# Dividing the attention probabilities by their row sums before they are transposed, on GpSimd and ScalarE, instead of scaling the output after the value product

## The chip, the cores and the metric

The kernel runs on one core of one Trainium2 chip, as one program and one launch. The metric is the device time of that core in microseconds, the lower the better; the time given for a kernel is the median of its runs. All five engines of the core take part: TensorE (PE in the rows; its weight loads are PEld), VectorE (DVE), ScalarE (ACT), GpSimd (POOL) and SyncE (SP, which only issues DMAs here).

## The reference, cut to what matters

The input is x, 2 batches of 512 tokens of width 256. The reference applies a layer norm with modulation, a first attention with a sliding window of 128 and sinks, a residual, a second layer norm with modulation, and then a block with a causal attention and a mixture of 8 experts (top 2). Both attentions have 32 query heads of width 64 in 8 groups of 4, each group sharing one key and one value head. The change touches the causal attention alone:

```
scores = einsum("bhqd,bhkd->bhqk", q, k) / sqrt(64)
scores = where(causal, scores, lowest)
attn = softmax(scores, axis=-1)            # exp, divided by the sum of the row
out = einsum("bhqk,bhkd->bhqd", attn, v)
return out.transpose(0, 2, 1, 3).reshape(b, s, 2048) @ wo
```

The division by the row's sum may be made on the probabilities (before the product with v) or on the output (behind it): a row of the output has one divisor per head, and both give the same numbers but for rounding.

## The kernel before

The attention is cut into 128 **units** u. A unit is one tile of 128 queries of one batch for the four heads of one group. Units 0 to 63 are the windowed attention, units 64 to 127 the causal one; `windowed(u)` tells them apart. Within four units the query tile t = u mod 4 runs from 0 to 3, and a causal unit has `keys(u)` = t + 1 blocks of 128 keys. Projections of the next groups (`ahead(u)`: q, k, v or features) are done between the units, in most steps of a segment but not in all; in the last twelve steps there are none.

Every engine has its own in-order program, written by hand as a loop over **steps**. In step u of the causal part (`step_causal`; `step` on GpSimd) the parts of several units are in flight:

- TensorE: `scores(u, j)` for the four heads j into psS; `turn_probs(u-2, k)` transposes the four heads' probabilities of key block k into psX; `values(u-2, k)` multiplies them with v into psO (its last block comes in the next step); `turn_scale(u-3)` transposes the two halves of rdenx into the other half of psO; `out_project(u-5)`; and `project(ahead(u))`. The first transposes of a step, `turn_probs(u-2, 0)`, come right behind `scores(u, 0)`.
- VectorE: `mask_max(u, j)` masks the scores, writes them to pbuf and takes the row's maximum; `probs_lo(u-2, k)` makes pTl, the low part of the transposed probabilities; `denominator(u-2)` takes the reciprocal of the sums (rden); `scale_out(u-3)` multiplies psO by rS into oS.
- ScalarE: `exp_head(u, j)` in place in pbuf with the row's sum; `probs_hi(u-2, k)` copies psX to pTh, the high part; `scale_of(u-3)` copies the transposed divisors to rS; `out_hi(u-4)` makes oh.
- GpSimd: `out_low(u-4)` makes ol = oS - oh; `low_weights(u)` makes the low part of the next weights; `spread(u-1)` copies rden four heads wide into rdenx; `gate_rows` in steps 84 to 88 is other work at the end of a step.

So a divisor takes this way before: reciprocal on VectorE, copy to 128x256 on GpSimd, two transposes on TensorE, a copy on ScalarE, and the multiplication on VectorE. The wait of `turn_probs(u, 0)` is for the four exponentials of its unit (a_exp), which ended a step earlier. Four buffers of probabilities (u mod 4) are in use in turn.

## Time and profile before

| | us |
|---|---|
| median of three runs | 1074.36 |
| the three runs | 1067.90, 1074.36, 1074.54 |
| the profiled execution | 1067.51 |
| its span, first to last instruction | 1065.9 |

In the profiled execution the causal steps run from about 407 to 800 us. Over the whole span TensorE is busy 91%, VectorE 74%, ScalarE 71% and GpSimd 44%. The granted clock of TensorE is given as a share of 2.4 GHz: 0.958 in the mean, 1.00 between 400 and 812 us. Times in the rows are microseconds from the span's start. A row of a timeline gives start and duration, engine, source line, operation, written tile <- read tiles and the number of merged instructions; in brackets stands the idle time of the engine just before it, and who ended it. Matmuls are pipelined, so that the duration of a row of four transposes (0.60) is longer than the time in which the next work can start (0.44 on the chain).

### The profile page before, as it was taken

The numbers are of one execution on the slowest core, as the hardware profiler recorded it, in microseconds if no ns is written. First come the engines' busy times: TensorE is split into PE (matmuls) and PEld (weight loads), VectorE is DVE, ScalarE is ACT, GpSimd is POOL, SyncE is SP. The second block draws the span as 40 slices with busy tenths as digits, with TensorE's granted clock in tenths as the row PEclk, the third lists the DMA queues.
The fourth block names the chain that finished last, engine by engine and source line by source line (L and its number), as shares of the span: only waits on it lengthen the run. The fifth ranks groups of instructions, "written<-read, shape, count | busy, mean of one in ns | idle before, by whom it ended". The sixth has DMA issues, their size and how long they took to land.

```text
span 1065.9 us, 22953 instructions
## 1 busy us (share of the span) xinstructions
PE 967.2 (91%) x6862; PEld 904.5 (85%) x6862; DVE 790.7 (74%) x2308; ACT 752.6 (71%) x2122; POOL 465.0 (44%) x550
## 2 busy tenths in 40 slices
PE   5679899999889899999999999999997689999991
PEld 3469899998789799988999999999987589999991
DVE  6679988889889677777776777677774766666646
ACT  3358787888788688788888778887784455665541
POOL 4347567868555443533354233222221862222243
PEclk9889999999999899999999999999998699999996
DMA  8789778896455586546456654645301385565314
GB/s 185 173 213 281 198 198 260 221 233 170 119 140 152 164 189 179 129 115 174 119 129 180 148 139 130 148 120 149 72 10 48 124 283 161 165 171 168 106 58 116
DMA packets 146059, 166.18 MB, mean 156 GB/s; under 512 B 79194, under 2 KB 100714, under 8 KB 140816
## 3 DMA queue, kind: packets, MB, share of 16 engines
q1 hardware_dynamic: 129440, 143.58, 52.1%
q0 software_dynamic: 3712, 11.16, 3.3%
q10 hardware_dynamic: 12784, 9.97, 3.0%
q8 instruction: 56, 0.92, 0.4%
q14 instruction: 67, 0.55, 0.2%
HBM read 105.88 MB, written 58.79 MB: 154 GB/s over the span
## 4 chain that ended last, share of the span: by engine, by line
PE 57%; DVE 18%; issue 9%; ACT 8%; DMA 3%; POOL 3%; SPq 0%; ACTq 0%; DVEq 0%; POOLq 0%
PE psO L1086 15%; PE psS L1053 10%; PE psX L1063 9%; PE psY L1102 6%; PE psP L985 6%; ACT wgt_hi L1319 3%; DVE pbuf L1735 3%; DVE gated L2065 2%; PE psO L1069 2%; PE psP L1015 2%; DVE pTl L1757 2%; POOL xg L892 2%; DVE den L1749 1%; PE psP L998 1%; DVE tmp L1703 1%
## 5 line engine op out<-in xcount | busy, mean ns | idle before, releaser
L1351 ACT ACTIVATE pbuf<-pbuf,nmax 128x256 f32<-128x256 f32 (+3 forms) x512 | 263.9, 517 | 45.6 <-DVE nmax L1735 44.7
L1053 PE MATMUL psS<-kT,qE 128*128 128x256 f32 (+3 forms) x1024 | 238.6, 317 | 27.0 <-DVE nmax L1735 25.4
L1735 DVE CUSTOM_DVE_ANT_0 pbuf<-psS,mcau 128x256 f32<-128x256 f32 (+3 forms) x512 | 219.4, 434 | 49.0 <-PE psS L1053 43.9
L1757 DVE TENSOR_TENSOR pTl<-psX,pTh 128x512 fp32r<-128x512 f32 x272 | 186.7, 686 | 75.2 <-ACT pTh L1319 74.6
L1319 ACT ACTIVATE pTh<-psX 128x512 fp32r<-128x512 f32 x272 | 160.3, 589 | 59.4 <-PE psO L1086 41.4
L1053 PEld LDWEIGHTS psS<-kT,qE 128*128 128x128 f32 x1024 | 161.4, 193 | 40.0 <-DVE nmax L1735 33.6
L1086 PE MATMUL psO<-pTh,vpad 128*128 128x256 f32 x1088 | 188.4, 296 | 4.8 <-DVE oS L1763 2.8
L798 POOL TENSOR_TENSOR ol<-oS,oh 128x256 fp32r<-128x256 f32 x128 | 94.8, 741 | 200.3 <-ACT oh L1319 195.8
L1063 PE MATMUL psX<-idn,pbuf 128*128 128x128 f32 x1088 | 163.6, 276 | 2.8 <-DVE pTl L1757 2.7
L1086 PEld LDWEIGHTS psO<-pTh,vpad 128*128 128x128 f32 x1088 | 151.2, 191 | 13.0 <-DVE oS L1763 6.6
L1063 PEld LDWEIGHTS psX<-idn,pbuf 128*128 128x128 f32 x1088 | 127.6, 142 | 9.1 <-DVE pTl L1757 3.2
L805 POOL COPY rdenx<-rden 128x256 f32<-128x256 f32 x128 | 50.9, 398 | 163.8 <-DVE rden L1752 127.9
L1086 PE MATMUL psO<-pTl,vpad 128*128 128x256 f32 x544 | 109.8, 283 | 0.0
L1351 ACT ACTIVATION_READ_ACCUMULATOR pbuf<-pbuf,nmax 128x1 f32 x512 | 98.4, 192 | 0.0
L1086 PEld LDWEIGHTS psO<-pTl,vpad 128*128 128x128 f32 x544 | 84.7, 191 | 0.0
L1102 PE MATMUL psY<-woh,oh 128*128 128x256 f32 x256 | 75.5, 295 | 3.1 <-POOL ol L798 3.1
L1319 ACT ACTIVATE hTh<-gated 128x320 fp32r<-128x320 f32 x64 | 30.2, 471 | 67.9 <-DVE gated L2065 67.9
L1102 PE MATMUL psY<-wol,oh 128*128 128x256 f32 x256 | 72.9, 285 | 0.0
L1102 PE MATMUL psY<-woh,ol 128*128 128x256 f32 x256 | 72.8, 284 | 0.0
L1319 ACT ACTIVATE rS<-psO 128x256 f32<-128x256 f32 x128 | 48.2, 377 | 24.7 <-PE psO L1069 23.7
L903 POOL TENSOR_TENSOR wgt_lo<-mrawB,wgt_hi 128x768 fp32r<-128x768 f32 x14 | 25.6, 1827 | 88.2 <-ACT wgt_hi L1319 87.9
L1763 DVE TENSOR_TENSOR oS<-psO,rS 128x256 f32<-128x256 f32 x128 | 53.6, 419 | 12.7 <-ACT rS L1319 10.7
(295 smaller groups left out, 2368.7 us busy)
## 6 DMA issues: line engine op xcount, KB each, us to landing
qd<-st SPq DMA_DIRECT2D x32, 1024.0 KB, 4.5
qE<-qd SPq DMA_DIRECT2D x128, 256.0 KB, 6.0
mrawV<-in_w_moe SPq DMA_DIRECT2D x32, 384.0 KB, 3.7
mrawB<-in_w_moe SPq DMA_DIRECT2D x32, 384.0 KB, 3.3
kT<-kd SPq DMA_DIRECT2D x64, 128.0 KB, 4.2
kT<-kd SPq DMA_DIRECT2D x32, 256.0 KB, 4.3
kd<-st SPq DMA_DIRECT2D x7, 1024.0 KB, 4.8
xg<-sq ACTq DMA_DIRECT2D x7, 640.0 KB, 4.8
```

The source lines that it names most:

```text
L798: G.tensor_tensor(ol[:, u % 2, :], oS[:, u % 2, :], oh[:, u % 2, :], ALU.subtract).then_inc(g_ol, 1)
L805: G.tensor_copy(rdenx[:, :].rearrange("p (h d) -> p h d", h=QM), rden[:, u % 4, :].unsqueeze(2).broadcast_to([P, QM, HD])).then_inc(g_rx, 1)
L985: last = mm(ps[:, :], w[:, g % 2, k, i * P:(i + 1) * P], a[:, k, b * SEQ:(b + 1) * SEQ], start=(n == 1), stop=(n == 3 * KC))
L1053: last = mm(psS[j % 2][:, 0:n], qE[:, g % 2, j, t * P:(t + 1) * P], kT[:, g % 2, c, k0:k0 + n], start=(c == 0), stop=(c == 1))
L1063: last = turn(psX[kt % 2][:, j * P:(j + 1) * P], probs(u, j)[:, k * P:(k + 1) * P], idn[:, :])
L1086: last = mm(psO[:, 0:2 * P], vpad[:, quad % 2, c, kv, at:at + 2 * HD], pairs(pT)[:, r], start=(k == 0 and n == 0), stop=(k == keys(u) - 1 ...
L1102: last = mm(psY[t // 2][:, t % 2 * D:(t % 2 + 1) * D], a[:, u % 2, i * P:(i + 1) * P], w[:, g % 2, i * D:(i + 1) * D], start=(first and n ...
L1319: copy = lambda o, i: nc.scalar.activation(o, i, ACT.Copy)
L1351: nc.scalar.activation(pj, pj, ACT.Exp, bias=nmax[:, u % 4, j:j + 1], scale=-1.0, accum_out=sums[:, u % 4, j:j + 1]).then_inc(a_exp, 1)
L1735: V.tensor_tensor_reduce(probs(u, j), psS[j % 2][:, 0:n], mcau[:, SEQ - n:], -SCALE, 3e38, ALU.add, ALU.min, nmax[:, u % 4, j:j + 1]).then ...
L1757: V.tensor_tensor(pTl[:, kt % 2, :], psX[kt % 2][:, :], pTh[:, kt % 2, :], ALU.subtract).then_inc(v_pl, 1)
L1763: V.tensor_tensor(oS[:, u % 2, :], psO[:, 0:2 * P], rS[:, u % 2, :], ALU.mult).then_inc(v_os, 1)
```

## The change

In the causal units the probabilities are divided in place in pbuf before they are transposed: heads 0 to 2 by GpSimd (`share_heads`, three multiplications by a column of rden), head 3 by ScalarE (`share_head`, a copy with that column as its scale). For this `denominator` of unit u-1 is done in step u, ahead of `mask_max(u, 2)`, where before unit u-2 had its turn behind `scale_out`. `turn_probs(u, 0)` waits for both engines (g_sc, a_sc). `spread`, `turn_scale` and `scale_of` are left out for these units, and `scale_out` becomes a plain copy. On GpSimd `out_low(u-4)` moves from the beginning of the step to behind `share_heads(u-1)`. The windowed units are unchanged. The declarations of the two semaphores are cut from the diff.

```diff
@@ -805,6 +807,14 @@
                 G.tensor_copy(rdenx[:, :].rearrange("p (h d) -> p h d", h=QM),
                               rden[:, u % 4, :].unsqueeze(2).broadcast_to([P, QM, HD])).then_inc(g_rx, 1)
 
+            def share_heads(u):
+
+                pool.wait_ge(v_rden, u + 1)
+                for j in range(QM - 1):
+                    apart(pool)
+                    last = G.tensor_scalar(probs(u, j), probs(u, j), rden[:, u % 4, j:j + 1], None, ALU.mult)
+                last.then_inc(g_sc, 1)
+
             def residual(t):
                 pool.wait_ge(v_ye, t + 1)
                 apart(pool)
@@ -829,7 +839,7 @@
 
             def step(u):
                 seg, r = divmod(u, SEGU)
-                if 0 <= u - 4 < NU:
+                if 0 <= u - 4 < NU and u <= 2 * SEGU:
                     out_low(u - 4)
                 if seg == 2 and 8 <= r < 20:
                     tables(r - 8)
@@ -842,7 +852,12 @@
                 if turns(u):
                     rope_sum(ahead(u)[:2])
                 if 0 <= u - 1 < NU:
-                    spread(u - 1)
+                    if windowed(u - 1):
+                        spread(u - 1)
+                    else:
+                        share_heads(u - 1)
+                if 2 * SEGU < u and u - 4 < NU:
+                    out_low(u - 4)
                 if u == SEGU - 1:
                     rows = yg.rearrange("(t p) d -> p t d", p=P)
                     first, end = (MAXT + 2) * 7 // 8, MAXT + 2
@@ -1056,8 +1071,11 @@
 
             def turn_probs(u, k):
                 kt = KT[u] + k + 1
-                if k == 0:
+                if k == 0 and windowed(u):
                     pe.wait_ge(a_exp, QM * (u + 1))
+                elif k == 0:
+                    pe.wait_ge(g_sc, u - 2 * SEGU + 1)
+                    pe.wait_ge(a_sc, u - 2 * SEGU + 1)
                 wait(pe, v_pl, kt - 2)
                 for j in range(QM):
                     last = turn(psX[kt % 2][:, j * P:(j + 1) * P], probs(u, j)[:, k * P:(k + 1) * P], idn[:, :])
@@ -1141,7 +1159,7 @@
                     values(u - 3, keys(u - 3) - 1)
                 if now:
                     scores(u, 2)
-                if u - 3 < NU:
+                if windowed(u - 3):
                     turn_scale(u - 3)
                 if nk > 1:
                     turn_probs(u - 2, 1)
@@ -1366,6 +1384,13 @@
                 act.wait_ge(s_rx, u + 1)
                 wait(act, v_os, u - 1)
                 copy(rS[:, u % 2, :], psO[:, 2 * P:4 * P]).then_inc(a_rx, 1)
+
+            def share_head(u):
+
+                act.wait_ge(v_rden, u + 1)
+                act.wait_ge(a_exp, QM * (u + 1))
+                pj = probs(u, QM - 1)
+                nc.scalar.activation(pj, pj, ACT.Copy, scale=rden[:, u % 4, QM - 1:QM]).then_inc(a_sc, 1)
 
             def out_hi(u):
                 act.wait_ge(v_os, u + 1)
@@ -1492,12 +1517,14 @@
                     probs_hi(u - 2, 0)
                 if now:
                     exp_head(u, 0)
-                if u - 3 < NU:
+                if windowed(u - 3):
                     scale_of(u - 3)
                 if now:
                     exp_head(u, 1)
                 if u == 2 * SEGU:
                     sink_exp(u - 1)
+                if u > 2 * SEGU and u - 1 < NU:
+                    share_head(u - 1)
                 if nk > 1:
                     probs_hi(u - 2, 1)
                 if now:
@@ -1759,6 +1786,9 @@
             def scale_out(u):
                 dve.wait_ge(s_PV, KT[u + 1])
                 wait(dve, g_ol, u - 1)
+                if not windowed(u):
+                    V.tensor_copy(oS[:, u % 2, :], psO[:, 0:2 * P]).then_inc(v_os, 1)
+                    return
                 dve.wait_ge(a_rx, u + 1)
                 V.tensor_tensor(oS[:, u % 2, :], psO[:, 0:2 * P], rS[:, u % 2, :], ALU.mult).then_inc(v_os, 1)
 
@@ -1851,11 +1881,15 @@
                     probs_lo(u - 2, 0)
                 if u == 2 * SEGU:
                     sink_in(u - 1)
+                if u == 2 * SEGU + 1:
+                    denominator(u - 2)
+                if u > 2 * SEGU and u - 1 < NU:
+                    denominator(u - 1)
                 if now:
                     mask_max(u, 2)
                 if u - 3 < NU:
                     scale_out(u - 3)
-                if u - 2 < NU:
+                if u == 2 * SEGU:
                     denominator(u - 2)
                 if nk > 1:
                     probs_lo(u - 2, 1)
```

How the instructions of three engines move is shown in their program order, near the end of the causal part (pbuf holds the probabilities, rden the reciprocals of their sums, wql and wol are low parts of weights). First GpSimd, from the division of a three-block unit to that of a four-block unit; before:

```order
L805 COPY rdenx<-rden 128x256 [waits v_rden,s_rx]
L798 TENSOR_TENSOR ol<-oS,oh 128x256 [waits a_oh]
L757 TENSOR_TENSOR wql<-wqraw,wqh 128x512 [waits a_wqh]
L805 COPY rdenx<-rden 128x256 [waits v_rden,s_rx]
L798 TENSOR_TENSOR ol<-oS,oh 128x256 [waits a_oh]
L767 TENSOR_TENSOR wol<-woraw,woh 128x512 [waits a_woh]
```

and now:

```order
L815 TENSOR_SCALAR pbuf<-pbuf,rden 128x384 [waits v_rden]
L815 TENSOR_SCALAR pbuf<-pbuf,rden 128x384 x2
L800 TENSOR_TENSOR ol<-oS,oh 128x256 [waits a_oh]
L759 TENSOR_TENSOR wql<-wqraw,wqh 128x512 [waits a_wqh]
L815 TENSOR_SCALAR pbuf<-pbuf,rden 128x512 [waits v_rden]
L815 TENSOR_SCALAR pbuf<-pbuf,rden 128x512 x2
L800 TENSOR_TENSOR ol<-oS,oh 128x256 [waits a_oh]
L769 TENSOR_TENSOR wol<-woraw,woh 128x512 [waits a_woh]
```

In place of one copy stand three multiplications as wide as the unit has keys, and ol stands in the same place of the row but belongs to the step of the multiplications ahead of it.

Next VectorE in the step whose own unit has three key blocks, before:

```order
L1735 ISA pbuf,nmax<-psS,mcau 128x384 [waits s_S]
L1735 ISA nmax 128x1
L1757 TENSOR_TENSOR pTl<-psX,pTh 128x512 [waits a_ph]
L1735 ISA pbuf,nmax<-psS,mcau 128x384 [waits s_S]
L1735 ISA nmax 128x1
L1763 TENSOR_TENSOR oS<-psO,rS 128x256 [waits a_rx,g_ol,s_PV]
L1752 RECIPROCAL rden<-sums 128x4 [waits a_exp]
```

and now:

```order
L1762 ISA pbuf,nmax<-psS,mcau 128x384 [waits s_S]
L1762 ISA nmax 128x1
L1784 TENSOR_TENSOR pTl<-psX,pTh 128x512 [waits a_ph]
L1779 RECIPROCAL rden<-sums 128x4 [waits a_exp]
L1762 ISA pbuf,nmax<-psS,mcau 128x384 [waits s_S]
L1762 ISA nmax 128x1
L1790 COPY oS<-psO 128x256 [waits g_ol,s_PV]
```

The reciprocal now follows pTl directly, and it is that of the unit one later.

Last TensorE at the beginning of the step whose own unit has four blocks, before:

```order
L1053 MATMUL psS<-kT,qE 128x512
L1063 MATMUL psX<-idn,pbuf 128x128 [waits v_pl,a_exp]
L1063 MATMUL psX<-idn,pbuf 128x128 x3
L1053 MATMUL psS<-kT,qE 128x512 [waits v_max]
```

and now:

```order
L1068 MATMUL psS<-kT,qE 128x512
L1081 MATMUL psX<-idn,pbuf 128x128 [waits v_pl,a_sc,g_sc]
L1081 MATMUL psX<-idn,pbuf 128x128 x3
L1068 MATMUL psS<-kT,qE 128x512 [waits v_max]
```

The place is the same; the wait is now for the divisions, with the rest of the step's matmuls queued behind it.

## Rows read from the trace of the kernel before

**Rows 1.** The page, part 1: busy time, share of the span, instructions.
```profile
PE 967.2 (91%) x6862; PEld 904.5 (85%) x6862; DVE 790.7 (74%) x2308; ACT 752.6 (71%) x2122; POOL 465.0 (44%) x550
```
**Rows 2.** The chain of waits from 409 to 800 us, by line.
```profile
by line: PE psO L1086 26.0%; PE psS L1053 18.1%; PE psX L1063 15.2%; PE psY L1102 10.6%; PE psP L985 9.0%; PE psO L1069 3.3%; issue 2.7%; DVE pbuf L1735 2.3%; PE psP L1015 2.2%; PE psP L998 2.1%; DVE pTl L1757 1.6%; ACT pTh L1319 1.2%; ACT 
```
**Rows 3.** Stretches: span, then busy PE, PEld, DVE, ACT, POOL, clock, DMA.
```profile
400.00:812.00 412.00, 403.50 (x3018) 378.00 (x3016) 299.41 (x927) 335.00 (x945) 137.47 (x203) 1.00 0.49 126
```
**Rows 4.** Timeline, TensorE: the first transposes of steps 64 and 128.
```profile
407.43 0.63 PE L1063 MATMUL psX<-idn,pbuf 128*128 128x128 f32 x4 [0.20 <-DVE pTl L1757]
...
800.14 0.60 PE L1063 MATMUL psX<-idn,pbuf 128*128 128x128 f32 x4
```
**Rows 5.** The same, steps 120 to 124: four steps without a projection.
```profile
756.45 0.62 PE L1063 MATMUL psX<-idn,pbuf 128*128 128x128 f32 x4
...
762.35 0.60 PE L1063 MATMUL psX<-idn,pbuf 128*128 128x128 f32 x4
...
769.57 0.60 PE L1063 MATMUL psX<-idn,pbuf 128*128 128x128 f32 x4
...
773.17 0.60 PE L1063 MATMUL psX<-idn,pbuf 128*128 128x128 f32 x4
...
778.38 0.62 PE L1063 MATMUL psX<-idn,pbuf 128*128 128x128 f32 x4
```
**Rows 6.** The same, steps 100 to 104: each of four steps has a projection.
```profile
633.00 0.62 PE L1063 MATMUL psX<-idn,pbuf 128*128 128x128 f32 x4
...
639.70 0.60 PE L1063 MATMUL psX<-idn,pbuf 128*128 128x128 f32 x4
...
647.43 0.60 PE L1063 MATMUL psX<-idn,pbuf 128*128 128x128 f32 x4
...
652.41 0.60 PE L1063 MATMUL psX<-idn,pbuf 128*128 128x128 f32 x4
...
658.61 0.62 PE L1063 MATMUL psX<-idn,pbuf 128*128 128x128 f32 x4
```
**Rows 7.** Timeline, first pTl of steps 100, 121, 122 and 123; reciprocal and spread of step 122.
```profile
634.38 0.69 DVE L1757 TENSOR_TENSOR pTl<-psX,pTh 128x512 fp32r<-128x512 f32 x1
...
763.68 0.69 DVE L1757 TENSOR_TENSOR pTl<-psX,pTh 128x512 fp32r<-128x512 f32 x1
...
771.15 0.69 DVE L1757 TENSOR_TENSOR pTl<-psX,pTh 128x512 fp32r<-128x512 f32 x1
...
772.70 0.17 DVE L1752 RECIPROCAL rden<-sums 128x4 f32<-128x4 f32 x1
...
773.02 0.40 POOL L805 COPY rdenx<-rden 128x256 f32<-128x256 f32 x1 [1.50 <-DVE rden L1752]
...
775.00 0.69 DVE L1757 TENSOR_TENSOR pTl<-psX,pTh 128x512 fp32r<-128x512 f32 x1
```
**Rows 8.** Groups by line and shape, GpSimd, 400 to 812 us: busy us, mean ns | idle.
```profile
L798 POOL TENSOR_TENSOR ol<-oS,oh 128x256 fp32r<-128x256 f32 x67 | 49.7, 743 | 165.8 <-ACT oh L1319 162.2 <-DVE yN L1771 3.6
L805 POOL COPY rdenx<-rden 128x256 f32<-128x256 f32 x68 | 27.0, 397 | 106.1 <-DVE rden L1752 101.4 <-PE psO L1069 4.7
...
L757 POOL TENSOR_TENSOR wql<-wqraw,wqh 128x512 fp32r<-128x512 f32 x13 | 16.8, 1292 | 0.5 <-POOL sinT L821 0.3 <-POOL sinT L817 0.2
...
L744 POOL TENSOR_SCALAR cB<-modb 128x512 f32<-128x512 f32 x1 | 1.9, 1935 | 0.0
...
L750 POOL TENSOR_SCALAR modb<-modb 128x512 f32<-128x512 f32 x1 | 1.5, 1490 | 0.0
...
L821 POOL TENSOR_SCALAR sinT<-sinT 128x128 f32<-128x128 f32 x1 | 0.5, 527 | 0.0
```
**Rows 9.** The same for ScalarE over the span.
```profile
L1319 ACT ACTIVATE rS<-psO 128x256 f32<-128x256 f32 x128 | 48.2, 377 | 24.7 <-PE psO L1069 23.7
...
L1319 ACT ACTIVATE woh<-woraw 128x512 fp32r<-128x512 f32 x32 | 19.9, 622 | 1.0 <-PE psY L1102 1.0
```
**Rows 10.** The chain that ended last, in order of time, step 122.
```profile
771.59 0.22 PE psO L1069 x2
```

More of the change, by code:

```diff
@@ L411, in build @@
         g_rx = sem("g_rx")
+        g_sc = sem("g_sc")
+        a_sc = sem("a_sc")
         s_mod = sem("s_mod")
```

## The prediction

> **What bounds the kernel now.** I read the page's busy shares first: TensorE is at 91% of the span, GpSimd at 44%, and nothing else is close to TensorE [rows 1]. Then the chain of waits over the causal part: TensorE's pieces make nearly nine tenths of it, of which the transposes of the divisors (psO, L1069) have 3.3% [rows 2]. GpSimd has room there in the sum: 137 of 412 us busy [rows 3]. So the engine that the change relieves is the one that bounds, and the one that it loads is two thirds idle. Whether that pays is decided by when GpSimd gets its work and when it must be done, and for this I looked at the timeline.
>
> As a clock I take the start of the first transposes of each step. From step 64 to step 128 it runs from 407.43 to 800.14 [rows 4]: 64 steps in 392.7 us. By the key blocks of the step's own unit (t = u mod 4) the steps last, in the mean of 16 each, 6.52 us (t = 0), 7.89 (t = 1), 4.36 (t = 2) and 5.77 (t = 3). Without projections they last 5.90, 7.22, 3.60 and 5.21 [rows 5], with one in each 6.70, 7.73, 4.98 and 6.20 [rows 6].
>
> **What is taken away.** Per causal unit TensorE loses two transposes, 0.22 us on the chain [rows 10]; 64 of them are **-14 us** if every step stays bound by TensorE. ScalarE loses the copy to rS, 0.38 us, and gets a copy of 128 to 512 columns; by the copy of 512 from SBUF, 0.62 [rows 9], that is about 0.3 to 0.6, so nearly even. It comes behind the second exponential of the step and is done before GpSimd: nothing. VectorE's multiplication becomes a copy of the same width from the same bank, and one reciprocal moves 0.2 us ahead of a mask; I cost both at nothing, since the next paragraphs keep TensorE waiting anyway. GpSimd loses its copy of 0.40 [rows 8].
>
> **What is added.** Three multiplications by a column on GpSimd per unit. The trace has no such instruction with a column as its factor; it has the one-operation form with a constant: 0.527 us for 128 columns and 1.490 for 512 [rows 8]. Along that line 256 columns take 0.85 and 384 take 1.17. Three heads of a unit with 1, 2, 3 or 4 blocks then take **1.58, 2.54, 3.51 and 4.47 us**. The bounds: the copy, 0.397 for 256 columns, as the cheap end (0.6, 1.2, 1.8, 2.4 in proportion), and the form with two operations, 1.935 for 512 (1.3 times my values), as the dear end [rows 8]. I take the one-operation form because it is the same instruction. GpSimd's sum grows by 16 x (12.1 - 1.6) = 168 us, to 305 of some 400: still no bound by its busy time.
>
> **The loop that the change closes.** In step u TensorE's first transposes are of unit u-2; ScalarE makes pTh and VectorE pTl; now the reciprocal of unit u-1 stands right behind that pTl; GpSimd divides unit u-1; and the first transposes of step u+1 wait for it. So the distance of two clock marks can't be less than this round. Its pieces: from the mark to the start of pTl 1.38 us (t = 0), 1.33 (t = 1), 1.58 (t = 2) and 1.83 (t = 3), where the growing part is the second mask, as wide as the step's unit [rows 5 to 7]; pTl 0.69; the reciprocal 0.17 and the step to GpSimd 0.15 (772.87 to 773.02) [rows 7]; the three multiplications; and 0.04 to TensorE. The unit divided in step t has 4, 1, 2 and 3 blocks. That gives
>
> - t = 0: 2.07 + 0.36 + 4.47 = **6.90** against 6.52 - 0.22,
> - t = 1: 2.02 + 0.36 + 1.58 = **3.96** against 7.89 - 0.22,
> - t = 2: 2.27 + 0.36 + 2.54 = **5.17** against 4.36 - 0.22,
> - t = 3: 2.52 + 0.36 + 3.51 = **6.39** against 5.77 - 0.22.
>
> Each step takes the larger of the round and its own old length less 0.22. For rows 5: +1.00, -0.22, +1.57, +1.18, so +3.5 us in 21.9. For rows 6: +0.20, -0.22, +0.19, +0.19, so +0.4 in 25.6. Done so for all 64 steps: **+6.1** (t = 0), **-3.5** (t = 1), **+13.4** (t = 2), **+9.9** (t = 3), together **+26 us**. The gain of 14 is inside this and is left whole only in the sixteen steps of t = 1. TensorE waits with a whole step's matmuls queued behind the transposes, and the time isn't made up later: the next round starts from the late mark.
>
> **Late starts on GpSimd.** The wide low part of the output (0.74) now stands behind the divisions and waits for oh, which ScalarE makes at the end of its step; then come the weights' low part (1.29) and the next divisions [rows 8]. In t = 0 steps with weights this is 0.74 + 1.29 behind a start some 0.5 us after the mark, 2.5 in all, against 2.4 when the reciprocal is there: about 0.1 to 0.2 in 12 steps, **+2**. At the end of step 87 the gate's maximum (1.49) stands in between as well, which puts step 88 about 1.2 late, and step 87 about 0.5: **+2**. What waits for ol has most of a step.
>
> **Sum.** +26 + 2 + 2 = **+30 us** on the profiled execution's 1067.5: 1097.5. Of the three runs shown one stands near the profiled one (1067.9) and two near 1074.4, and which of the two the new runs will show I can't tell; I take the middle, +3, and forecast **1100 us**. A measurement of this kernel can tell about 1% from no change.
>
> **Rivals.**
>
> *GpSimd multiplies at the rate of its copy.* Then the rounds are 4.8, 3.0, 3.8 and 4.7 us, below nearly every step of TensorE; only six bare t = 2 steps stay some 0.4 longer than TensorE needs. The sum is -14 + 2 = -12: 1056 to 1062, about 1059, faster. For it: one tensor is read, as in the copy. Against it: the constant forms read one tensor as well, and take 1.9 times as long for 512 columns as the copy would in proportion (1.490 against 0.794) [rows 8]. The Trainium skill, GPSIMD Engine Reference, "Engine selection", calls GpSimd's elementwise work with one input roughly line-rate, which would be this rival. By that rule the trace disagrees: its one-input form takes 2.9 ns per column, so the rival gets little. **0.14**. The point from which it decides: with my fixed times the sum passes zero where the multiplications cost 0.78 of what I take, a four-block unit 3.5 us.
>
> *The loop closes, but is short enough.* Multiplications at 0.7 to 0.9 of the row: the long steps with projections hide them, the bare ones pay, and the two sides cancel: -4 to +10, so 1064 to 1083. For it: in rows 6 the margins are 0.2 us each, so that a small error of the fixed times turns eight or nine tens of steps. Against it: those fixed times are rows of this trace. **0.12**.
>
> *The factor from memory is dear.* At 1.3 times the row (the two-operation form) the rounds are 8.2, 4.4, 5.9 and 7.4, and the sum is +76: about 1150. **0.06**.
>
> My forecast, with the multiplications within a tenth of the row's price (+10 to +42 by the same sum, and the late starts): 1080 to 1115. **0.68**.
>
> **Range and chances.** 1062 to 1118 holds the forecast, the second rival and the upper edge of the first, and leaves out most of the first and the third. Faster by over 1%, so below 1063: most of the first rival, 0.11. Within 1%: the second and the rest of the first, 0.15. Slower by over 1%: 0.74.
>
> **What would show it.** L815 on GpSimd: 192 instructions, with means near 0.53, 0.85, 1.17 and 1.49 us by width, and GpSimd near 300 us busy in the causal part. TensorE idle before the psX transposes of about 40 steps, released by GpSimd's pbuf, 1 us or more in bare t = 2 steps and none in t = 1. The distances of the marks at the end of the causal part 6.9, 7.0, 5.2 and 6.4. In the chain of waits GpSimd's pbuf instead of psO L1069, and pTh, pTl and the reciprocal with larger shares. The windowed part and the experts as before. Wrong would be: L815 at 0.4 for 256 columns (first rival); the waits there, but the marks no farther apart (my addition of round and step is wrong); a causal part longer by 30 us without waits on GpSimd's pbuf, for instance by ScalarE's division or by a lower granted clock, which is 1.00 there now [rows 3].

## The result, and the profile after

| | before | after |
|---|---|---|
| median, us | 1074.45 (4 runs, 1067.9 to 1075.45) | 1102.63 (4 runs, 1100.35 to 1109.41) |
| ratio after/before, 95% interval | | 1.0322 [1.0277, 1.0367] |
| profiled execution, its span | 1067.51, 1065.9 | 1100.35, 1098.8 |
| first transposes of step 64 and step 128 | 407.43, 800.14 | 408.68, 836.32 |

The forecast was 1100 (1062 to 1118), slower. Of the 32.9 us by which the span grew, 34.9 lie between the two marks of the causal part; 1.3 came ahead of them and 3.3 went behind them, where the change does nothing: the stretch behind the second mark lasted 265.7 us at a granted clock of 0.91 before and 262.5 at 0.92 after. Over the whole span the clock is 0.958 in the mean in both.

The ratio is the one on record; the quotient of the two medians is 1.026. Both are clearly slower, and the account below goes by the traces.

The page of the changed kernel, part 1: busy time, share of the span, instructions.

```profile
PE 961.2 (87%) x6734; PEld 889.9 (81%) x6734; DVE 785.4 (71%) x2308; ACT 769.5 (70%) x2122; POOL 645.6 (59%) x678
```

Against [rows 1] TensorE has 128 instructions fewer and GpSimd 181 us more. The groups by shape on GpSimd, 400 to 850 us (busy us, mean ns | idle before them), which answer to [rows 8]:

```profile
L815 POOL TENSOR_SCALAR pbuf<-pbuf,rden 128x512 f32<-128x512 f32 x48 | 74.5, 1567 | 9.7 <-DVE rden L1779 9.6
L815 POOL TENSOR_SCALAR pbuf<-pbuf,rden 128x384 f32<-128x384 f32 x48 | 59.1, 1246 | 27.2 <-DVE rden L1779 27.2
L800 POOL TENSOR_TENSOR ol<-oS,oh 128x256 fp32r<-128x256 f32 x68 | 50.2, 738 | 58.0 <-ACT oh L1337 57.2
L815 POOL TENSOR_SCALAR pbuf<-pbuf,rden 128x256 f32<-128x256 f32 x48 | 44.1, 934 | 19.6 <-DVE rden L1779 19.6
L815 POOL TENSOR_SCALAR pbuf<-pbuf,rden 128x128 f32<-128x128 f32 x48 | 28.4, 607 | 3.7 <-DVE rden L1779 3.6
```

The price of a multiplication lies on a straight line, 0.607 to 1.567 us, which is 0.08 above the form with a constant at both ends. The Trainium skill, GPSIMD Engine Reference, "Engine selection", calls one-input elementwise work roughly line-rate; these rows disagree: a multiplication of 256 columns takes 0.934 us where the plain copy took 0.397 [rows 8], and each further column costs 2.5 ns. The last column says the other half: GpSimd still sits idle for the reciprocal ahead of its divisions, least ahead of the 128 and 512 wide ones. It isn't short of time in the sum, it gets its work late.

The waits of TensorE in the same window (us in total, times, longest), and the chain of waits from 409 to 830 us by line, which answers to [rows 2]:

```profile
PE psX L1081 <- POOL pbuf L815: 41.5, 48, 2.2
PE psO L1104 <- DVE pTl L1784: 3.1, 6, 0.7
```
```profile
by line: POOL pbuf L815 36.7%; PE psX L1081 11.9%; PE psO L1104 10.4%; issue 6.6%; PE psS L1068 6.3%; DVE pTl L1784 4.7%; DVE pbuf L1762 4.5%; PE psP L1000 3.0%; ACT pTh L1337 2.4%; PE psY L1120 2.0%; DVE rden L1779 1.6%; ACT pbuf L1369 1.2
```

The same chain in order of time over two steps without a projection (start, us, what), t = 2 and then t = 3. Each round begins with psX and psS, and goes on over a mask:

```profile
798.83 0.44 PE psX L1081 x4
799.26 0.36 PE psS L1068 x2
...
799.76 0.56 DVE pbuf L1762
...
800.33 0.41 DVE pTl L1784
...
800.85 0.18 DVE rden L1779
...
801.19 2.74 POOL pbuf L815 x3
...
803.97 0.66 PE psX L1081 x4
804.63 0.48 PE psS L1068 x2
...
805.24 0.69 DVE pbuf L1762
805.93 0.01 DVE nmax L1762
805.94 0.39 DVE pTl L1784
...
806.46 0.18 DVE rden L1779
...
806.80 3.70 POOL pbuf L815 x3
```

This is the round that the prediction drew: transposes, scores, mask, pTl, reciprocal, divisions, and at once the next transposes. The timeline of TensorE has the marks of steps 122 to 125, in brackets what it waited for:

```profile
798.66 0.60 PE L1081 MATMUL psX<-idn,pbuf 128*128 128x128 f32 x4
...
803.97 0.66 PE L1081 MATMUL psX<-idn,pbuf 128*128 128x128 f32 x4 [1.72 <-POOL pbuf L815]
...
810.54 0.66 PE L1081 MATMUL psX<-idn,pbuf 128*128 128x128 f32 x4 [1.07 <-POOL pbuf L815]
...
817.53 0.66 PE L1081 MATMUL psX<-idn,pbuf 128*128 128x128 f32 x4 [0.93 <-POOL pbuf L815]
```

Step by step, with the forecast round beside it (us; the sum is over the 16 steps of a kind, from the marks of both traces):

| t | bare step before | after | forecast | mean before | mean after | sum | forecast |
|---|---|---|---|---|---|---|---|
| 0 | 5.90 | 6.98 | 6.90 | 6.52 | 7.20 | +10.8 | +6.1, and up to +4 for late starts |
| 1 | 7.22 | 6.91 | 7.00 | 7.89 | 7.54 | -5.7 | -3.5 |
| 2 | 3.60 | 5.31 | 5.17 | 4.36 | 5.39 | +16.5 | +13.4 |
| 3 | 5.21 | 6.58 | 6.39 | 5.77 | 6.61 | +13.3 | +9.9 |

The waits on GpSimd stand in 15 steps of t = 0, all of t = 2 and of t = 3, and of t = 1 in step 65 alone (0.09 us).

### The profile page after: what moved, and what is told of

Its sections match the earlier page's. It is cut to its first block, busy times and chain, and to the rows that moved or that the text cites. A ratio compares the mean times of both kernels' runs of the same rounds, so it can differ in the third digit from the quotient of the medians.

```text
span 1098.8 us, 22822 instructions
## 1 busy us (share of the span) xinstructions
PE 961.2 (87%) x6734; PEld 889.9 (81%) x6734; DVE 785.4 (71%) x2308; ACT 769.5 (70%) x2122; POOL 645.6 (59%) x678
## 4 chain that ended last, share of the span: by engine, by line
PE 39%; DVE 20%; POOL 17%; issue 10%; ACT 10%; DMA 2%; DVEq 0%; SPq 0%; ACTq 0%; POOLq 0%
POOL pbuf L815 14%; PE psO L1104 9%; PE psX L1081 8%; PE psS L1068 6%; PE psP L1000 4%; DVE pbuf L1762 3%; PE psY L1120 3%; ACT wgt_hi L1337 3%; DVE pTl L1784 3%; DVE gated L2099 2%; PE psS L1254 2%; ACT relu_s L1652 1%; PE psX L1254 1%; DVE den L1776 1%; PE psP L1030 1%
## 5 line engine op out<-in xcount | busy, mean ns | idle before, releaser
L1068 PE MATMUL psS<-kT,qE 128*128 128x256 f32 (+3 forms) x1024 | 235.8, 317 | 24.7 <-DVE nmax L1762 23.2
L815 POOL TENSOR_SCALAR pbuf<-pbuf,rden 128x128 f32<-128x128 f32 (+2 forms) x192 | 206.0, 1089 | 60.2 <-DVE rden L1779 59.9
L1081 PE MATMUL psX<-idn,pbuf 128*128 128x128 f32 x1088 | 165.9, 278 | 43.0 <-POOL pbuf L815 41.5
L1081 PEld LDWEIGHTS psX<-idn,pbuf 128*128 128x128 f32 x1088 | 125.2, 142 | 61.7 <-POOL pbuf L815 54.4
L807 POOL COPY rdenx<-rden 128x256 f32<-128x256 f32 x64 | 25.7, 401 | 67.5 <-PE psO L1087 39.1
L2101 DVE TENSOR_TENSOR hTl<-gated,hTh 128x320 fp32r<-128x320 f32 x64 | 34.5, 540 | 34.5 <-ACT hTh L1337 31.8
```

The costliest lines, as they stand in the source:

```text
L815: last = G.tensor_scalar(probs(u, j), probs(u, j), rden[:, u % 4, j:j + 1], None, ALU.mult)
L1068: last = mm(psS[j % 2][:, 0:n], qE[:, g % 2, j, t * P:(t + 1) * P], kT[:, g % 2, c, k0:k0 + n], start=(c == 0), stop=(c == 1))
L1081: last = turn(psX[kt % 2][:, j * P:(j + 1) * P], probs(u, j)[:, k * P:(k + 1) * P], idn[:, :])
L2101: V.tensor_tensor(gTl[:, f % NR, :], gated[:, f % 2, :], gTh[:, f % NR, :], ALU.subtract).then_inc(m_gl, 1)
```

## The experiments

The theory: the round closes over GpSimd, and a step lasts as long as the longer of the round and TensorE's own work. The rivals that were put up against it: the change costs because GpSimd has more to do; because ScalarE divides too; because the transposes moved or the masks came later; because GpSimd's low part came late. The table gives each median, its ratio to the kernel before with the interval, the four sums (t = 0, 1, 2, 3, from the marks against those of before), and the last bare steps. Each experiment's ratio is taken with runs of before on the same chip. The experiments ran on four chips, so that a small difference between two of their ratios says little; the sums between the marks are the finer measure.

| kernel | median | ratio | sums, us | bare t = 0, 1, 2, 3 |
|---|---|---|---|---|
| after | 1102.63 | 1.0322 [1.0277, 1.0367] | +10.8, -5.7, +16.5, +13.3 | 6.98, 6.91, 5.31, 6.58 |
| e1_one_column | 1064.08 | 0.9963 [0.9937, 0.999] | +0.5, -3.9, -2.9, -1.4 | 6.40, 6.84, 3.43, 5.28 |
| e2_low_first | 1507.53 | 1.411 [1.4047, 1.4173] | +136.3, +84.0, +102.2, +109.3 | 12.1, 12.5, 9.5, 12.0 |
| e3_early_reciprocal | 1083.73 | 1.0125 [1.0084, 1.0166] | +15.7, -6.4, +3.4, +0.9 | 6.57, 6.86, 3.95, 5.27 |
| e4_two_and_two | 1086.62 | 1.018 [1.0133, 1.0227] | +14.5, -3.8, +4.0, -0.2 | 7.15, 7.14, 4.40, 5.35 |
| e5_double_one_block | 1107.24 | 1.0373 [1.0312, 1.0434] | +10.6, -3.5, +16.4, +13.2 | 6.97, 6.91, 5.30, 6.57 |
| e6_double_two_blocks | 1159.34 | 1.086 [1.0799, 1.0921] | +12.8, -6.4, +57.5, +27.1 | 6.98, 6.91, 8.01, 7.42 |
| e7_both_early | 1069.41 | 1.0026 [0.9991, 1.0061] | +10.7, -5.2, +0.8, +0.2 | 6.10, 7.12, 3.95, 5.27 |
| e8_room_for_both | 1063.91 | 0.9978 [0.9944, 1.0012] | -3.0, -0.6, +1.8, -0.5 | 5.61, 6.88, 3.98, 5.25 |
| e9_one_column_share_late | 1061.76 | 0.9907 [0.9876, 0.9939] | -4.2, -4.0, +1.6, -1.5 | 5.38, 6.71, 4.05, 5.31 |
| e10_weights_behind | 1060.78 | 0.9905 [0.987, 0.994] | -3.1, -3.4, +1.9, -0.5 | 5.60, 6.88, 3.98, 5.23 |
| e11_reciprocal_first | 1062.93 | 0.9932 [0.9896, 0.9968] | -3.0, -3.4, +1.9, -0.7 | 5.61, 6.88, 3.98, 5.26 |
| e12_both_shares_in_time | 1063.99 | 0.9907 [0.9876, 0.9937] | -2.8, -3.4, -0.9, +0.1 | 5.69, 6.89, 3.37, 5.23 |

Each edit is shown against the changed kernel, or against the experiment that it starts from.

### e1_one_column: the divisions without their width

```diff
-                    last = G.tensor_scalar(probs(u, j), probs(u, j), rden[:, u % 4, j:j + 1], None, ALU.mult)
+                    pj = probs(u, j)[:, 0:1]
+                    last = G.tensor_scalar(pj, pj, rden[:, u % 4, j:j + 1], None, ALU.mult)
```

> GpSimd multiplies one column of each head in place of all (the other columns stay undivided, and the output is not the reference's); order, waits and ScalarE's division as in the changed kernel. Theory (the round through GpSimd's three wide multiplications sets the distance of the steps): an instruction of one column takes about 0.25 us, so the rounds shrink to 2.3 + 0.8 to 2.9 + 0.8, below every step of TensorE. The bare steps last 5.7, 7.0, 3.4 and 5.0 (t = 0 to 3), the idle time of TensorE in front of the transposes that GpSimd releases is under 3 us in all, and the time is about 1050 us on a run like the profiled one, 1045 to 1062. Rival (the cost lies in ScalarE's division, in the reciprocal's new place ahead of a mask, or in the longer chain of semaphores): it stays above 1080.

The kernel leaves out the division of all columns but one, so its time shows what the width costs and nothing more.

All waits on GpSimd's pbuf went, and with them 42.6 us between the marks (385.03 against 427.65): the width of GpSimd's divisions is what costs, and not the new order of VectorE. 1064.08 is 2 us above the expected range (1045 to 1062), and most of what is missing lies in t = 0. The timeline of its step 120 shows where (ScalarE, and TensorE's marks):

```profile
749.12 0.62 PE L1082 MATMUL psX<-idn,pbuf 128*128 128x128 f32 x4
...
750.68 0.62 PE L1082 MATMUL psX<-idn,pbuf 128*128 128x128 f32 x4
...
751.76 0.72 ACT L1394 ACTIVATE pbuf<-pbuf,rden 128x512 f32<-128x512 f32 x1
752.39 0.58 ACT L1338 ACTIVATE pTh<-psX 128x512 fp32r<-128x512 f32 x1
...
755.52 0.60 PE L1082 MATMUL psX<-idn,pbuf 128*128 128x128 f32 x4
```

The second transposes are done at 751.3, but pTh of them begins at 752.39, behind the division of a four-block unit (0.72). The prediction cost ScalarE's part at nothing because GpSimd would be later still; once that cover is gone it looks worth 0.7 us in each bare t = 0 step: 6.40 where TensorE's own work is 5.68. e9 below tests this.

### e2_low_first: the output's low part back in front

```diff
-                if 0 <= u - 4 < NU and u <= 2 * SEGU:
+                if 0 <= u - 4 < NU:
                     out_low(u - 4)
...
-                if 2 * SEGU < u and u - 4 < NU:
-                    out_low(u - 4)
```

> The changed kernel with the output's low part back at the beginning of GpSimd's step, where the kernel before has it. The divisions then stand behind the wait for oh, which ScalarE makes as the last thing of its step. Theory: the round becomes mark to oh (5.1, 6.9, 4.7 and 6.3 us for t = 0 to 3 in the changed kernel's trace), 0.9 for ol and the step to GpSimd, and the divisions (4.65, 1.77, 2.73, 3.69): 10.7, 9.6, 8.3 and 10.9 against 6.98, 6.91, 5.31 and 6.58, so about 14 us per four steps or 150 to 230 us in all: 1250 to 1330. Rival (the order is of no account, since GpSimd is idle for a third of the time anyway): 1095 to 1110.

The direction was right, the size too small (1507.53 for 1250 to 1330). oh is made at the end of a step, so with ol ahead of them the divisions begin only there, and the step and the divisions add up instead of overlapping: 9.5 to 12.9 us for a bare step. On top of that the granted clock was 0.77 between 409 and 836 us, where it was 1.00 in the changed kernel. So the second part of the change, ol last, is what makes the first bearable. It doesn't cost, it saves some 400 us. How much of these is the lower clock, and how much the longer round, isn't separated here.

### e3_early_reciprocal: the round made shorter

```diff
                     mask_max(u, 0)
+                if u > 2 * SEGU and u - 1 < NU:
+                    denominator(u - 1)
...
-                if u > 2 * SEGU and u - 1 < NU:
-                    denominator(u - 1)
                 if now:
                     mask_max(u, 2)
```

> The changed kernel with the reciprocal of unit u-1 right behind the first mask of step u, ahead of the second mask and of the first low part. It needs the last exponential of unit u-1 alone, which ends between 0.6 us before and 0.9 us after the mark. Theory: what makes the round is that the reciprocal waits behind pTl, which waits for the transposes. With it ahead of them the divisions start about 0.7 to 1.3 us after the mark in place of 2.3 to 2.8, and what is left is GpSimd's own sum: bare steps 5.9, 7.0, 3.8 and 5.0 to 5.2, in steps with weights some tenths more. Total: the changed kernel less 30 to 45 us, about 1055 to 1072 on a run like the profiled one. Rival (GpSimd's busy time is the cost wherever it stands, the SBUF or the engine being in the way): less than 10 us gained.

t = 2 and t = 3 behaved: bare steps of 5.31 went to 3.95 and of 6.58 to 5.27, and the two kinds lost 25.5 us together. t = 0 grew, to 15.7 above before, so that 21.4 us are left between the marks and 1083.73 lies above the expected 1055 to 1072. Its step 112, which has weights (GpSimd, oh, and the marks of steps 112 and 113):

```profile
719.48 0.62 PE L1081 MATMUL psX<-idn,pbuf 128*128 128x128 f32 x4
720.11 0.40 ACT L1337 ACTIVATE oh<-oS 128x256 fp32r<-128x256 f32 x1
...
720.66 0.73 POOL L800 TENSOR_TENSOR ol<-oS,oh 128x256 fp32r<-128x256 f32 x1 [1.38 <-ACT oh L1337]
...
721.36 1.29 POOL L759 TENSOR_TENSOR wql<-wqraw,wqh 128x512 fp32r<-128x512 f32 x1
722.62 4.65 POOL L815 TENSOR_SCALAR pbuf<-pbuf,rden 128x512 f32<-128x512 f32 x3
...
727.33 0.44 PE L1081 MATMUL psX<-idn,pbuf 128*128 128x128 f32 x2 [1.20 <-POOL pbuf L815]
```

The two marks are 7.85 apart. ol can't start before oh, wql follows it, and so the divisions began 3.14 us after the mark and ended at 7.79. With the reciprocal early, GpSimd's own queue is what delays the divisions. The prediction named this kind of late start and put it at 2 us; at the old place of the reciprocal it was hidden behind the reciprocal.

### e4_two_and_two: a head taken from GpSimd and given to ScalarE

```diff
-                for j in range(QM - 1):
+                for j in range(QM - 2):
...
-                pj = probs(u, QM - 1)
-                nc.scalar.activation(pj, pj, ACT.Copy, scale=rden[:, u % 4, QM - 1:QM]).then_inc(a_sc, 1)
+                for j in (QM - 2, QM - 1):
+                    pj = probs(u, j)
+                    last = nc.scalar.activation(pj, pj, ACT.Copy, scale=rden[:, u % 4, j:j + 1])
+                last.then_inc(a_sc, 1)
```

> The changed kernel with two heads divided by ScalarE and two by GpSimd. Theory: GpSimd's part of the round falls by a third: 3.1, 1.2, 1.85 and 2.5 us, the rounds to 5.4, 3.4, 4.3 and 5.3, so that only the bare t = 2 steps and a few t = 3 ones exceed TensorE. ScalarE gets 0.3 to 0.6 us more per step ahead of the second pTh. 1060 to 1078. Rival (ScalarE's division costs as much on the path as GpSimd's): 1090 or more.

A third of GpSimd's divisions is gone, and 20.4 of the 34.9 us between the marks with it. 1086.62 lies between what the theory (1060 to 1078) and the rival (1090 or more) expected. The waits of TensorE, 400 to 830 us:

```profile
PE psO L1104 <- DVE pTl L1786: 15.4, 21, 1.3
PE psX L1081 <- POOL pbuf L815: 6.2, 13, 0.8
```

A new wait took the place of the old one: two divisions (1.4 us in t = 0) stand ahead of the second pTh, pTl follows late, and the value products wait. Bare t = 0 is 7.15, longer than in the changed kernel.

### e5_double_one_block and e6_double_two_blocks: the same load in a step with room and in one without

```diff
                 pool.wait_ge(v_rden, u + 1)
+                if u >= 2 * SEGU + 4 and u % 4 == 0:
+                    for j in range(QM - 1):
+                        apart(pool)
+                        G.tensor_scalar((rdenx[:, 0:128], rS[:, 0, 0:128], rS[:, 1, 0:128])[j], probs(u, j), rden[:, u % 4, j:j + 1], None, ALU.mult)
```

The second has `u % 4 == 1` and 256 columns. The extra multiplications write to buffers that nothing reads there.

> The changed kernel with GpSimd's work doubled for the 15 one-block units from unit 68 on (three more multiplications of 128 columns into scratch, ahead of the real ones): 1.8 us more in each t = 1 step. Theory (each step takes the longer of its round and TensorE's own length): the round of t = 1 grows from 4.1 to 5.9 us, still below 6.9 to 7.9, so nothing: within 2 us of the changed kernel, ratio to the kernel before 1.030 to 1.034. Rival (GpSimd's work adds up wherever it stands): 15 x 1.8 = 27 us more, ratio 1.057.

> The same for the 15 two-block units from unit 69 on (three more multiplications of 256 columns): 2.75 us more in each t = 2 step, whose round already sets its length. Theory: these steps grow from 5.3 to 8.1 us, and nothing comes back in the next one: 38 to 42 us more than the changed kernel, ratio to the kernel before 1.067 to 1.073. Rival (time lost in one step is made up in the long t = 1 steps): under 20 us more.

In 15 steps of t = 1 GpSimd did 1.77 us more each, 27 us in all, and between the marks the kernel was 1.8 longer (429.47 against 427.65), bare t = 1 steps 6.91 as in the changed kernel. All but two of the 15 steps have the same length as there. Step 85 is 0.5 us longer; GpSimd has the gate's work in front of its divisions there. Step 89 is 1.6 longer, and this is the clock: first e5, then the same two stretches of the changed kernel, the wait at the end of step 88 and what follows (columns as below).

```profile
574.36:576.55 2.19, 0.00 (x1) 0.00 (x1) 0.43 (x3) 0.49 (x1) 2.19 (x3) 1.00 1.07 210
576.55:579.83 3.28, 3.28 (x20) 3.28 (x21) 1.89 (x7) 2.09 (x7) 3.11 (x3) 0.69 1.13 212
```
```profile
576.70:578.90 2.20, 0.00 (x1) 0.01 (x1) 0.43 (x2) 0.49 (x1) 2.20 (x3) 1.00 1.08 210
578.90:582.18 3.28, 3.28 (x24) 3.12 (x25) 1.94 (x8) 2.59 (x8) 3.11 (x3) 1.00 1.13 212
```

The wait is the same, and the clock fell behind it in one execution and not in the other. The ratio, 1.0373, is above the expected 1.034; the traces give no more than the 1.8 us for it.

So GpSimd's busy time cost nothing in 13 of the 15 steps; where the round is the longer one it counts. In 15 steps of t = 2 the extra 2.7 us came in whole (+41 between the marks, 5.31 to 8.01). But t = 3 also grew by 14, which neither side had expected. Stretches of e6: a t = 2 step up to TensorE's wait, the wait, and what follows (span, then busy PE, PEld, DVE, ACT, POOL, clock, DMA share, GB/s):

```profile
815.71:819.30 3.59, 3.43 (x25) 2.97 (x22) 3.08 (x11) 3.02 (x9) 1.75 (x3) 1.00 0.01 5
819.30:823.72 4.42, 0.16 (x1) 0.16 (x2) 0.70 (x2) 0.91 (x3) 4.42 (x6) 0.87 0.00 0
823.72:827.00 3.28, 3.28 (x13) 3.03 (x14) 1.32 (x4) 1.89 (x4) 0.48 (x1) 0.50 0.00 0
827.00:831.14 4.14, 4.14 (x23) 3.58 (x22) 2.40 (x7) 2.66 (x7) 3.69 (x3) 0.71 0.08 16
```

and the same wait in the changed kernel:

```profile
776.50:778.21 1.71, 0.02 (x1) 0.02 (x1) 0.70 (x2) 1.02 (x3) 1.71 (x3) 1.00 0.00 0
778.21:784.79 6.58, 5.08 (x35) 4.26 (x35) 3.90 (x12) 4.94 (x12) 4.38 (x5) 1.00 0.27 74
```

After 4.42 us almost idle TensorE was granted 0.50, its lower level of 1.2 GHz, over the next 3.28 us; after 1.71 us idle it kept 1.00, which is 2.4 GHz. Shorter waits of e6 did the same: behind the 3.10 us at the end of step 70 the next 3.28 us had 0.51, behind the 3.08 of step 86 they had 0.66. So these waits are paid twice. The changed kernel, whose longest wait is 2.2 us, had 1.00 from the first mark to the second. The median, 1159.34, is 8.6% above before, where 6.7 to 7.3% was expected.

### e7_both_early, e8_room_for_both, e10_weights_behind: mending the three late starts

e7 is e3 with oh made early in ScalarE's step, so that ol has left GpSimd before the reciprocal comes:

```diff
+                if u - 4 < NU:
+                    out_hi(u - 4)
                 if now:
                     exp_head(u, 1)
...
-                if u - 4 < NU:
-                    out_hi(u - 4)
                 between(u)
```

> The kernel with the early reciprocal, and in addition ScalarE makes oh behind its first exponential of the step in place of last, so that GpSimd's low part of the output, now behind the divisions, no longer waits for it. Theory: in the run with the early reciprocal the t = 0 steps with weights last 7.7 to 7.9 us, since GpSimd begins the four-block divisions only when oh, ol (0.74) and the weights' low part (1.3) are done. With oh early the weights' part starts at about 0.6 us after the mark, the divisions at 1.9, and they end at 6.6: t = 0 steps of 6.6 to 6.8, 8 to 14 us less than with the early reciprocal alone, ratio to the kernel before 0.999 to 1.006. Rival (what is left over there comes from ScalarE's division ahead of the second pTh): under 3 us less.

The ratio is as expected, but the t = 0 steps with weights are not: step 112 lasts 7.55 where 6.6 to 6.8 was expected, and its divisions start 2.83 us after the mark, not 1.9. t = 0 still had +10.7. Two causes were left to try, ScalarE's division ahead of the second pTh and the weights ahead of the divisions. e8 takes both away, the division behind the third exponential and wql from the t = 0 to the t = 1 steps:

```diff
-                    if m == at and 4 * quad + part < NG:
+                    if m == at + (u > 2 * SEGU) and 4 * quad + part < NG and u != 2 * SEGU:
                         low_wq(4 * quad + part)
...
-                if u > 2 * SEGU and u - 1 < NU:
-                    share_head(u - 1)
                 if nk > 1:
                     probs_hi(u - 2, 1)
                 if now:
                     exp_head(u, 2)
+                if u > 2 * SEGU and u - 1 < NU:
+                    share_head(u - 1)
```

> The last one, and in addition the low part of the q weights moves from the t = 0 step to the next (t = 1), where GpSimd has room, and ScalarE's division moves behind the third exponential, past the second pTh. Theory: both things that are left on the t = 0 steps go: TensorE's own 5.7 (bare) to 6.5 us (with a projection) come through, t = 1 gives 0.3 to 0.4 us, t = 2 and t = 3 about as before. Causal part 5 to 12 us shorter than in the kernel before, ratio 0.988 to 0.996. Rival (GpSimd is now the bound by its sum, about 19 us in 22 to 25, and any order leaves waits): ratio 1.00 or more.

t = 0 fell to -3.0 (bare 5.61), by both edits together; only for ScalarE's division does e9 give a price of its own. The whole is 2.3 us below before between the marks, where 5 to 12 was expected, because some t = 1 steps lost. In steps 73 and 77 the value products waited 1.3 and 1.4 us for pTl, which I did not follow up (0.4 and 0.7 in the changed kernel). Two others were longer than before: step 65, 6.89 instead of 5.69, and step 109, 10.19 instead of 8.62. In step 65 GpSimd made wql and wol (2.6 us) ahead of the divisions, and the next transposes waited 1.03 us for these. The timeline at step 109:

```profile
685.11 1.30 POOL L759 TENSOR_TENSOR wql<-wqraw,wqh 128x512 fp32r<-128x512 f32 x1
...
685.71 2.38 DVE L1847 SCALAR_TENSOR_TENSOR hb<-yN,rs,ln_b 128x256 f32<-128x256 f32 x2
...
686.39 1.42 POOL L769 TENSOR_TENSOR wol<-woraw,woh 128x512 fp32r<-128x512 f32 x1
```

The two instructions that make hb, the normalised input of the next projections, took 2.38 us beside wql and wol; in e10, where GpSimd does neither at that moment, the same two take 0.88:

```profile
687.41 0.88 DVE L1850 SCALAR_TENSOR_TENSOR hb<-yN,rs,ln_b 128x256 f32<-128x256 f32 x2
```

The Trainium skill, SBUF — State Buffer, "Who interferes with whom", says that a VectorE instruction with two inputs in SBUF contends with a GpSimd instruction that reads SBUF. These rows agree in that the overlap costs: 1.50 us for two instructions. e10 is e8 with the weights of the t = 1 steps behind the divisions and ol, and those of step 64 left there:

```diff
-                    if m == at + (u > 2 * SEGU) and 4 * quad + part < NG and u != 2 * SEGU:
+                    if m == at + (u > 2 * SEGU + 1) and 4 * quad + part < NG:
                         low_wq(4 * quad + part)
...
-                if u < NU:
+                behind = u > 2 * SEGU + 1 and u % 4 == 1
+                if u < NU and not behind:
                     low_weights(u)
...
                     out_low(u - 4)
+                if u < NU and behind:
+                    low_weights(u)
```

> The kernel with room for both, in which step 65 lasted 1.2 and step 109 1.6 us longer than in the kernel before. In step 109 two of VectorE's instructions with two SBUF inputs (hb) took 0.98 and 1.49 us beside GpSimd's wql and wol, against 0.48 in the mean before. Here the weights' low parts stand behind the divisions and ol in the t = 1 steps, and those of step 64 stay where they were. Theory: hb runs beside nothing, step 109 returns to about 8.4, step 65 to 5.7: 2.5 to 3.5 us less, ratio to the kernel before 0.992 to 0.997. Rival (step 109 waits for a DMA of that run alone): no change in it.

Step 109 is 8.67 and step 65 5.69, and between the marks e10 is 2.8 us shorter than e8, as expected. By the ratio, 0.9905 [0.987, 0.994], this version is 4% faster than the changed kernel (0.9905/1.0322) and 0.95%, some 10 us, faster than before; that is clear of 1, but under the 2% from which the record calls a kernel faster. Its trace shows half of this: 387.63 us between the marks against 392.71. The rest of its profiled execution, the slowest of its eight runs, does not: the stretch behind the marks lasted 272.2 us at a clock of 0.89, against 265.7 at 0.91 before. Where the other 5 us come from is open.

### e9_one_column_share_late: is it ScalarE's division in t = 0?

e1 with the division behind the third exponential, as in e8:

```diff
-                if u > 2 * SEGU and u - 1 < NU:
-                    share_head(u - 1)
                 if nk > 1:
                     probs_hi(u - 2, 1)
                 if now:
                     exp_head(u, 2)
+                if u > 2 * SEGU and u - 1 < NU:
+                    share_head(u - 1)
```

> The run with one column per head on GpSimd (the other columns of heads 0 to 2 stay undivided, so the output is not the reference's), with ScalarE's division moved behind the third exponential. In the first of these the t = 0 steps kept 6.40 us (bare) where TensorE alone needs 5.68, and no wait on GpSimd is left to explain it. Theory: ScalarE's four-block division (0.7 us) stands ahead of the second pTh, and the values wait for it. Now bare t = 0 steps of 5.6 to 5.7, t = 0 in the sum 4 to 8 us less than with one column alone, ratio to the kernel before 0.985 to 0.992: this is the most that the change could have given. Rival (the reciprocal's place, or the copy that takes the multiplication's place on VectorE): 6.3 or more.

Bare t = 0 went from e1's 6.40 to 5.38: the 0.7 us named in e1, and 0.3 more, which I can't account for. t = 2 rose from 3.43 to 4.05, since there the third exponential ends just before the next transposes: the same place is right in one kind of step and late in another.

### e11_reciprocal_first and e12_both_shares_in_time: what holds t = 2

e11 is e10 with the reciprocal ahead of the first mask in t = 2 steps; e12 is e11 with ScalarE's division in those steps back behind the second exponential.

```diff
-                if now:
+                if now and u % 4 != 2:
                     mask_max(u, 0)
...
+                if now and u % 4 == 2:
+                    mask_max(u, 0)
```
```diff
+                if u > 2 * SEGU and u - 1 < NU and u % 4 == 2:
+                    share_head(u - 1)
                 if nk > 1:
                     probs_hi(u - 2, 1)
                 if now:
                     exp_head(u, 2)
-                if u > 2 * SEGU and u - 1 < NU:
+                if u > 2 * SEGU and u - 1 < NU and u % 4 != 2:
                     share_head(u - 1)
```

> The last one, and in the t = 2 steps the reciprocal stands ahead of the first mask as well: its unit's last exponential has ended 0.6 us before the mark there. Theory: the bare and nearly bare t = 2 steps of 3.95 to 4.3 us are GpSimd's 2.73 behind a reciprocal at 1.03; with it ahead, GpSimd starts at 0.7, when its ol is done: 3.5, 0.4 us less in about ten steps, so 3 to 5 us less, ratio to the kernel before 0.988 to 0.994. Rival (the first mask, and with it the first exponential, is then late by the reciprocal and costs as much): ratio as the last one.

> The kernel with the reciprocal first, where the bare t = 2 steps stayed at 3.98 us although GpSimd's divisions end at 2.73 us after the mark: ScalarE's own, behind its third exponential, ends at 3.88. Here it stands behind the second exponential again in the t = 2 steps alone (they have no second pTh that it could delay). Theory: it ends at about 3.3, TensorE's own length of 3.4 comes through: bare t = 2 steps of 3.4 to 3.5, t = 2 in the sum 3 to 6 us less than in the last one, ratio to the kernel before 0.986 to 0.992. Rival (the wait is still one for GpSimd, or for the first pTh): 3.9 or more, ratio 0.99 to 0.995.

My theory on e11 fell: t = 2 stayed at 3.98, though GpSimd was done 2.7 us after the mark. Its step 122:

```profile
764.16 2.73 POOL L815 TENSOR_SCALAR pbuf<-pbuf,rden 128x256 f32<-128x256 f32 x3 [2.35 <-DVE rden L1782]
...
767.55 0.50 ACT L1396 ACTIVATE pbuf<-pbuf,rden 128x256 f32<-128x256 f32 x1
...
768.15 0.52 PE L1084 MATMUL psX<-idn,pbuf 128*128 128x128 f32 x3 [0.45 <-issue]
```

ScalarE's division now ends last, at 768.05. In e12 it is in time, and the step is 3.37, before's 3.60 less the removed transposes:

```profile
761.91 0.50 ACT L1396 ACTIVATE pbuf<-pbuf,rden 128x256 f32<-128x256 f32 x1
...
762.64 0.60 PE L1084 MATMUL psX<-idn,pbuf 128*128 128x128 f32 x4
```

That took 2.8 us off the sum of t = 2 and 1.8 off the whole between the marks, but the three ratios of e10, e11 and e12, 0.9905, 0.9932 and 0.9907, can't be told apart.

## Why the prediction was right, point by point

- **The removed transposes, -14.** The 0.22 per unit is right, the 14 is not reached, since some steps are not bound by TensorE. e12 has the round open in nearly all steps and lies 7.0 us below before between its marks. Most steps are shorter by 0.2, but t = 2 has only -0.9 in the sum (steps 66, 82 and 98 are longer) and t = 3 nothing (75, 79 and 83 are 0.3 to 0.4 longer). Bare t = 3 steps of e12 stay at 5.2: TensorE does the transposes' time less and waits instead, for VectorE's copy to oS, which empties psO for the next value products.

```profile
766.16 0.74 PE L1107 MATMUL psO<-pTh,vpad 128*128 128x256 f32 x4 [0.37 <-DVE oS L1795]
```

That copy ends at 766.11, behind the masks. These products start 3.52 us after the mark here and 3.51 before, so VectorE's order already set that part of the step.
- **The multiplications, 1.58 to 4.47 per unit.** Low by 0.18 each: 1.77, 2.73, 3.69 and 4.65. The factor from memory costs 0.08 per instruction over the constant form [rows 8]; the widths were right along the line.
- **The fixed part of the round, 2.43, 2.63 and 2.88.** Measured 2.27, 2.52 and 2.83 from the mark to the first division (t = 0, 2, 3; for step 122 798.66 to 801.19 above), and 0.05 from the last division to the mark: 2.32, 2.57 and 2.88, lower by 0.11, 0.06 and nothing; why I did not follow up. It took back part of the miss above: rounds of 6.98, 5.31 and 6.58 for 6.90, 5.17 and 6.39, 6.5 us over 48 steps.
- **Longer of round and own length, +26.** Held in kind: bare and projected steps have the same length after (6.98 in both at t = 0), and the one wait in t = 1 is 0.09. e5 and e6 test the same rule from the other side. 48 waits, where about 40 were forecast (the forecast's own rounds are the longer ones in 46 steps).
- **t = 1, -3.5.** Measured -5.7. Bare steps gave 0.31 instead of 0.22, and four long ones (69, 73, 77, 109) 0.7 to 1.1 each. Before, TensorE waited in 69 and 109 for the mask's maximum (0.48 and 0.35) and in 73 and 77 for VectorE's multiplication to oS (0.93 and 0.90), which in turn waited 1.25 us for rS in both. Step 73 before:

```profile
467.48 0.74 PE L1086 MATMUL psO<-pTh,vpad 128*128 128x256 f32 x4 [0.93 <-DVE oS L1763]
```

  After, TensorE waits in 73 and 77 for pTl, 0.41 and 0.74 us, and in 69 and 109 for nothing. So in 73 and 77 the whole way of the divisor was on the path, where the prediction took only its two transposes off; for 69 and 109 the cause is open.
- **Late starts, +2 and +2.** Partly. Step 88 is 8.26, 1.3 above the round, as forecast (1.2). Step 87 isn't late. In the steps with weights nothing of the 0.1 to 0.2 is seen (step 112: 6.99), but steps 68 and 76 are 1.1 and 0.6 late. Together 3.3 in t = 0, and another 1 in t = 2.
- **ScalarE and VectorE, nothing.** True in this kernel, and only in its cover. e1 and e9 put ScalarE's division at 0.7 to 1.0 us per bare t = 0 step once GpSimd isn't later.
- **Sum.** 34.9 between the marks for 30; 32.8 on the profiled execution; 28.2 between the medians. That 1102.63 lies so near 1100 is in part luck: the sum was 4.9 too low between the marks, the stretches outside them, where the change does nothing, gave back 2.0, and the +3 was the middle of two values. The range would have held without this luck.

The rivals: the copy's rate would give 1.8 us for three heads of a three-block unit where 3.69 stands, and is out; the short round is out by the same rows; the dear factor is true in kind but costs 1.05 times the row for 512 columns and 1.15 for 128, not 1.3.

## What to carry to other kernels

Before a piece of work goes to an idle engine, draw the round it closes: from the event that gives it its input to the event that waits for its output, with every mask, copy and reciprocal on the way. Idle time in the sum says nothing: 1.8 us more on GpSimd was free in most steps of one kind, and in another 2.7 us more cost 2.7. When such a round is too long, the order inside the step is the cheap remedy: here the same work, in other places of three queues, went from 3.2% slower to 0.95% faster by the ratios (34.9 us longer to 5.1 shorter between the marks), and each step that was mended brought the next engine's late piece to light.

## What the runs showed of the hardware

- After 4.42 us with TensorE 0.16 us busy the granted clock was 0.50 in the next 3.28 us (e6); 1.71 us idle left it at 1.00. After 2.19 us idle it was 0.69 over the next 3.28 us in e5, after 2.20 us 1.00 in the changed kernel.
- GpSimd's multiplication with a column from memory: 0.607, 0.934, 1.246 and 1.567 us for 128 to 512 columns; 0.286 for one column (e1).
- Two VectorE instructions with two SBUF inputs took 2.38 us beside two of GpSimd, 0.88 without.
